# A gated attention layer and an expert layer on one core: the first stage's features and gather done by halves, the second half's projections moved into the next stage, and the unread products ahead of the first weights left out

## The reference

```python
# layer 1: attention with 16 heads of 64, gated by a top-32 choice of tokens
q, k, v = split(x @ w_qkv.T, 3)                     # INNER = 1024 each
dots = einsum('bhid,bhjd->bhij', q, k) * 64 ** -0.5
f = layernorm(q.mean(heads)) * ln_g + ln_b          # q_mean: 64 features a token
scores = gelu(f @ w1.T + b1) @ w2.T + b2            # one number a token
gate = sigmoid(scores where in the top 32 of its batch, else -1e9)   # else 0
attn = softmax(dots * gate[:, None, :, None] * gate[:, None, None, :])
x = layernorm(x + (attn @ v) @ w_out.T + b_out)

# layer 2: causal attention with 16 heads of 8, then 8 experts, top 2
x1 = x + mla(rmsnorm(x) * g1)                       # causal softmax
h = rmsnorm(x1) * g2
logits = h @ gate_w; combine = softmax of the top 2 of 8
y = x1 + sum_e combine[e] * (silu(h @ w1[e]) @ w2[e])
x = layernorm(x + y)
```

## Time and profile before

| | us |
|---|---|
| median of 3 timed runs | 706.88 |
| the 3 runs | 701.70, 706.88, 715.31 |
| the profiled execution, its own time | 699.82 |
| its span, first to last instruction | 698.1 |
| PE busy | 645.9 (93%) |
| DVE, ACT, POOL busy | 491.2, 419.5, 256.5 |
| end of the first block (the copy of delta on DVE) | 73.8 |
| mean granted clock of TensorE | 0.976 |

### The profile page before, as it was taken

The page is one execution under the profiler, slowest core; times in us unless marked ns, Lnnn a source line. Parts: engine busy times, 40 slices in busy tenths (PEclk is TensorE's granted clock), DMA queues, the critical chain, the costliest instruction groups (busy, mean ns, idle before and its releaser), DMA issues.

```text
span 698.1 us, 13992 instructions
## 1 busy us (share of the span) xinstructions
PE 645.9 (93%) x5388; PEld 429.9 (62%) x5388; DVE 491.2 (70%) x1043; ACT 419.5 (60%) x753; POOL 256.5 (37%) x321
## 2 busy tenths in 40 slices
PE   7689689889899999999999999999999999989985
PEld 2367444455456666666666766767676667756765
DVE  2557456865777778877887788768777877764775
ACT  2543254666577666766685768666857575664432
POOL 3632301221243344343532543343334343533433
PEclk9899798999999999999999999999999999999999
DMA  8500000000000000000000000000000000000000
GB/s 318 178 0 32 1 1 1 2 1 1 1 1 2 1 1 1 16 2 1 1 17 1 1 2 16 1 1 3 16 1 1 2 17 1 1 1 16 1 16 15
DMA packets 9923, 12.15 MB, mean 17 GB/s; under 512 B 1593, under 2 KB 8194, under 8 KB 9602
## 3 DMA queue, kind: packets, MB, share of 16 engines
q1 hardware_dynamic: 9106, 11.25, 4.8%
q10 hardware_dynamic: 752, 0.01, 0.1%
HBM read 9.16 MB, written 2.10 MB: 16 GB/s over the span
## 4 chain that ended last, share of the span: by engine, by line
PE 69%; DVE 10%; ACT 5%; issue 3%; POOL 2%; POOLq 0%; ACTq 0%; DVEq 0%
PE turn L964 15%; PE turn L957 11%; PE psV L1017 11%; PE psW L1005 9%; PE psS L990 6%; PE turn L919 5%; PE turn L909 3%; DVE negmax L1198 3%; PE psS L979 2%; ACT prob L1117 2%; PE turn L927 2%; ACT X L1036 1%; PE turn L938 1%; DVE qs L1207 1%; PE turn L872 1%
## 5 line engine op out<-in xcount | busy, mean ns | idle before, releaser
L1117 ACT ACTIVATE prob<-psW 128x1024 f32<-128x1024 f32 (+1 forms) x192 | 182.9, 953 | 109.5 <-PE psW L1005 109.1
L1198 DVE TENSOR_REDUCE negmax<-psS 128x2 f32<-128x1024 f32 (+2 forms) x249 | 198.7, 818 | 31.5 <-PE psS L990 31.0
L841 POOL TENSOR_SCALAR_AFFINE_SELECT prob<-prob 128x512 f32<-128x512 f32 x128 | 80.0, 638 | 280.0 <-ACT prob L1117 280.0
L1258 DVE SCALAR_TENSOR_TENSOR late<-late,turn 128x512 f32<-128x512 f32 x128 | 87.5, 684 | 66.3 <-ACT late L1087 65.6
L964 PE MATMUL turn<-wexp,late 128*128 128x128 f32 x1024 | 128.0, 278 | 1.5 <-DVE late L1258 1.3
L964 PEld LDWEIGHTS turn<-wexp,late 128*128 128x128 f32 x1024 | 119.6, 192 | 9.6 <-issue 6.0
L1087 ACT ACTIVATE late<-turn 128x512 f32<-128x512 f32 x128 | 76.4, 598 | 60.7 <-PE turn L957 57.9
L1005 PE MATMUL psW<-qT,kT 26*128 26x256 f32 (+2 forms) x512 | 93.1, 400 | 8.9 <-ACT prob L1117 8.1
L849 POOL TENSOR_TENSOR late<-late 128x512 f32<-128x512 f32 x63 | 80.6, 1280 | 45.7 <-DVE late L1277 45.7
L979 PE MATMUL psS<-kT,qT 24*128 24x256 f32 (+1 forms) x498 | 90.7, 400 | 1.7 <-DVE negmax L1198 1.6
L1017 PE MATMUL psV<-prob,va 128*32 128x512 f32 (+3 forms) x1024 | 91.0, 450 | 0.2 <-POOL prob L841 0.2
(11 more groups left out here) (260 smaller groups left out, 900.8 us busy)
## 6 DMA issues: line engine op xcount, KB each, us to landing
XT<-in_xT SPq DMA_DIRECT2D x4, 512.0 KB, 6.7
X<-in_x SPq DMA_DIRECT2D x1, 2048.0 KB, 15.8
out<-late SPq DMA_DIRECT2D x8, 256.0 KB, 2.2
WQKV<-in_wqkvT SPq DMA_DIRECT2D x1, 1024.0 KB
late<-in_w SPq DMA_DIRECT2D x1, 1024.0 KB, 9.6
WQKV<-in_wqkvT SPq DMA_DIRECT2D x2, 256.0 KB, 3.7
late<-in_woutT SPq DMA_DIRECT2D x1, 512.0 KB
base_all<-base_rows SPq DMA_DIRECT2D x1, 512.0 KB, 3.8
```

Of the source, the lines that this page charges most:

```text
L841: pool.affine_select(out=blk, in_=blk, compare_op=ALU.is_ge, fill=0.0, base=0, pattern=[[0, 4], [1, P]], channel_multiplier=-1).then_inc(s ...
L1117: A(into, src, ACT.Exp).then_inc(s["exp_ready"], 1)
L1198: last = V.tensor_reduce(negmax[:, u % 2, c, 2 * p:2 * p + 2], scores_in(b, n)[:, :, HALF * i:HALF * i + P * (c + 1)], AX, ALU.max, negate ...
L1258: V.scalar_tensor_tensor(out=hid[:, e % 2, k, :], in0=tanh[:, n % 2, :], scalar=1.0, in1=bank("hidden", b, n)[:, :], op0=ALU.add, op1=ALU. ...
```

## The change

First block:

- **Features by halves.** `features`, the copies, squares, variances and gate rows go by 256 tokens of each batch: eight steps t (first halves of all batches, then second halves) in place of four. The first half's variance, root and reciprocal run while the second half's products are made. w1g waits for three of the small loads only (`ld_w1`); the other four are waited for later (`ld_gate`). A root table is loaded ahead on ACT. 12 unread products (IN_GATE) stand on PE behind the transposes of the value weights and ahead of the scores' product.
- **Split gather.** Half 0 is gathered (16 of the 32 multiplications, L331 before), then its base rows, queries, keys and scores follow; half 1 is gathered after those scores. ACT copies its Xg and xm, and its base rows have a product, a copy and two DMAs of their own. POOL adds batches 3, 5, 6 and 7, DVE the other four.
- **The other half's projections** (16 query and key multiplications, 2 of values) leave the first block, with the 10 unread products at L377. They become six steps `half parts` between `apply` of batch 0 and `apply` of batch 1 in the second block, in the rotation of the three turn banks, emptied by ACT. For that WQKV, XT, Xg and Xc lie in the memory of `prob`, which the second block first writes at its first weights.

Second block: 11 of the 28 places in UNREAD_AT go, all those below 0; some places in the tables are moved by 0.2 to 2 slots; the last two experts' sums of the last batch are done on DVE alone (it was the last one only).

```diff
-            for j in range(B // 2):
-                if j >= 1 and j + 1 < B // 2:
-                    features(j + 1)
-
-                pe.wait_ge(f_sb, 2 * j + 2)
-                mm(bank[6][rows_of(j), :], ones64[:, :], sq[:, j % 2, :], start=True, stop=True,
+            for t in range(B):
+                h, j = divmod(t, B // 2)
+                if t >= 1 and t + 1 < B:
+                    features(t + 1)
+
+                pe.wait_ge(f_sb, 2 * t + 2)
+                mm(var_in[h][rows_of(j), 0:HALF], ones64[:, :], sq[:, t % 2, 0:HALF], start=True, stop=True,
                    tile_position=(0, 2 * GH * j)).then_inc(v_done, 1)
...
+            pe.wait_ge(masks, 2)
+            pe.wait_ge(g_used, 1)
+            unread(IN_GATE)
...
+            gather(0)
+            pe.wait_ge(xs_sb, 1)
+            base_rows(0)
...
+            pe.wait_ge(w1_scaled, 1)
+            gather(1)
...
-            values(0, (bank[7], bank[5]))
-            other = [bank[k] for k in (2, 3, 0, 1)]
-            queries_keys(1, other, range(2))
-            pe.wait_ge(s_shift, 1)
-            queries_keys(1, other, range(2, 4))
-
-            pe.wait_ge(qk1_sb, 1)
-            for i in range(IN_SOFTMAX):
-                mm(bank[2][:, :], keep["identb"][:, :], keep["maskb"][:, :], start=True, stop=True)
+            pe.wait_ge(xm_ready, 1)
+            base_rows(1)
...
-            dve.wait_ge(ld_gate, 16 * 5)
-            dve.wait_ge(ld_zero, 32)
-            dve.wait_ge(consts, 1)
-            V_.tensor_scalar(w1g[:, :], w1raw[:, :], gcol[:, :], None, ALU.mult)
-            V_.tensor_scalar(w2sel[:, :], w2sel[:, :], w2col[:, :], None, ALU.mult).then_inc(wc_ready, 1)
+            dve.wait_ge(ld_w1, 16 * 3)
+            V_.tensor_scalar(w1g[:, :], w1raw[:, :], gcol[:, :], None, ALU.mult).then_inc(w1_ready, 1)
...
+            for n in range(NH):
+                rows = slice(HB * n, HB * n + HB)
+                sp.wait_ge(base_sb, n + 1)
+                sp.dma_start(keep["rows"][rows, :], base[:, n, :]).then_inc(base_out[n], 16)
+                sp.wait_ge(base_out[n], 16)
+                sp.dma_start(base_all[:, rows, :], keep["rows"][rows, :].unsqueeze(0).broadcast_to([P, HB, D])
+                             ).then_inc(base_in[n], 16)
...
+WARM, IN_GATE, BY_POOL = 7, 12, (3, 5, 6, 7)
...
-OF_GROUP = {"keys": -12.05, "queries": -13.6, "shift": -4.1, "again": -3.1, "values": -6.75}
+OF_GROUP = {"keys": -12.05, "queries": -13.4, "shift": -4.1, "again": -3.45, "values": -5.4}
...
-GATE_AT, SUM_AT, ADD_AT = 1.0, 1.21, 2.02
+GATE_AT, SUM_AT, ADD_AT = 1.0, 1.21, 1.32
...
+    ("half parts", 0): -40.25, ("half parts", 1): -40.15, ("half parts", 2): -40.05, ("half parts", 3): -39.95,
...
 UNREAD_AT = [
-    -11.2, -10.2, -9.2, -8.2, -7.2, -6.2, -5.2, -4.2, -2.2, -1.2, -0.2, 1.8, 3.8, 5.8, 7.8, 9.8, 11.8, 13.8, 15.8,
...
-                    if (b, n) == (B - 1, NE - 1):
+                    if b == B - 1 and n >= NE - 2:
```

More of the change, by code:

```diff
@@ L298, in _ @@
             last.then_inc(wvo_ps, 1)
-            pe.wait_ge(ld_next, 16 * len(keep["loads"]))
-            mm(bank[5][:, 0:2 * D], keep["wd"][:, :], keep["wu"][:, :, :], start=True, stop=True).then_inc(wqk_ps, 1)
-            def unread(count):
-                for i in range(count):
-                    mm(bank[6][:, :], keep["identb"][:, :], keep["maskb"][:, :], start=True, stop=True)
-            pe.wait_ge(masks, 2)
             for i in range(TOPK // 8):
@@ L312, in _ @@
             unread(6)
+            pe.wait_ge(ld_next, 16 * len(keep["loads"]))
+            mm(bank[5][:, 0:2 * D], keep["wd"][:, :], keep["wu"][:, :, :], start=True, stop=True).then_inc(wqk_ps, 1)
             pe.wait_ge(wvo_sb, 1)
@@ L350, in _, with gather @@
[L350 to L353 removed]
+            def gather(n):
+                pe.wait_ge(gr_ready, n + 1)
+                for b in range(HB * n, HB * n + HB):
+                    o = (2 * TOPK + 1) * (b % HB)
+                    for c in range(C):
+                        last = mm(bank[4 + n][:, o:o + 2 * TOPK + 1], X[:, C * b + c, :], GR[:, C * b + c, :],
+                                  start=(c == 0), stop=(c == C - 1))
+                last.then_inc(xs_ps, 1)
@@ L887, in _ @@
                     pe.wait_ge(s["half_T"], 2)
+                    for i in range(4, 6):
+                        wait_free(pe, "half parts", 0, i)
                     for k in range(H):
```

301 lines of the change are left out of this document (161 added, 140 removed).

## The result

| | before | after |
|---|---|---|
| median, us (15 runs each) | 706.88 | 698.05 |
| lowest and highest | 700.40, 715.31 | 696.30, 699.49 |
| the profiled execution, own time | 699.82 | 698.13 |
| its span | 698.1 | 696.0 |
| mean granted clock | 0.976 | 0.969 |

The ratio of the times is 0.9903, 95% interval 0.9879 to 0.9927: 6.9 us less (5.2 to 8.6) at 706.88 us. The longest executions of the kernel before, over 1.5% above its fastest, are left out of this ratio and not of the median. The two profiled executions differ by 2.1 us of span only, since the one of before was shorter than all of its timed runs.

A forecast was written before the change was run, and what follows sets the result against it. PE was read as busy almost throughout from 200 us, so gains must come ahead of the first weights at 110 us, plus the tail. Terms 3.7 + 3.7 - 0.7 + 0 + 2.3 + 0.4 = 9.4 us gave 697.5 us, range 687 to 706.

The forecast's parts named there:

- Gate stage: Start to scores on DVE: features by halves, loads decide, scores at 26.1 us against 29.78; 3.7 us gained.
- upper end: Gate stage: the bias lands before X, so the scores come at 24.5 us; a gain of 5.3 us.
- Split gather: First block: all 64 gather passes took 7.33 us, the path now has 32 of them; 3.7 us gained.
- End of the block: First block's end, old clock: POOL's additions end it at 74.5 us, not 73.8; 0.7 us lost.
- The six new steps: Second block's start: moved projections covered by PE's idle time; 0, bounds 1.3 us lost and 1.5 gained.
- the clock stays low: Lower bound for the six new steps at the second block's start: 1.3 us lost.
- Unread products: Between scores and first weights: 22 products go, PE keeps 12.7 us of work; 2.3 us gained.
- the clock falls between the scores: Rival, from the first scores on: a lower clock takes the 2.3 us back; 4.4 gained, 702.5 us, chance 0.17.
- Tail: Last experts' sums: DVE's sum no longer stands behind POOL's addition; 0.4 us gained.
- Tables: Moved places of steps and POOL's additions: PE does the same work, so 0, up to 5 us gained.
- more than the sum: Rival, long stretch: PE's waits of 7.2 and 3.9 us go by half; 14.9 gained, 692 us, chance 0.22.
- So I subtract the same gain from the median: Whole kernel: the 9.4 us taken off the profiled execution (690.4 us) also come off the median (697.5 us).

The follow-up runs named there:

- a_no_gate: The changed kernel without the 12 unread products ahead of the scores' product (IN_GATE = 0); median 696.53 us, ratio 0.9879 to the kernel before.
- a_gather_whole: The changed kernel with the gather of half 1 put back directly behind that of half 0; median 699.3 us, ratio 0.9937 to the kernel before.
- a_share: The changed kernel with batch 7's base row added by DVE and not by POOL; median 697.25 us, ratio 0.9873 to the kernel before.
- a_apply_first: The changed kernel with apply of batch 1 ahead of the six half parts; median 697.0 us, ratio 0.9898 to the kernel before.
- b_unread_out: The kernel before without its 11 places of unread products ahead of the first weights; median 710.02 us, ratio 1.0083 to the kernel before.
- a_unread_back: The changed kernel with the 11 places of unread products put back; median 693.38 us, ratio 0.9823 to the kernel before.
- c_three: The changed kernel with the 11 unread places back, IN_GATE = 0 and batch 7 added by DVE; median 693.16 us, ratio 0.9850 to the kernel before.
- a_tables_old: The changed kernel with the old places in the tables and of the additions; median 701.07 us, ratio 0.9980 to the kernel before.
- b_again: The kernel before run once more, unchanged; median 705.3 us, ratio 0.9986, profiled execution 712.11 us.
- b_warm: The kernel before with ten unread products in place of six behind the last round of the top 32; median 702.61 us, ratio 0.9981.
- b_two_covers: The kernel before with its two PE waits of the gate stage covered by unread products; median 702.66 us, ratio 0.9964.
- a_warm_end: The changed kernel with 14 unread products behind the last product of the first block; median 697.27 us, ratio 0.9885 to the kernel before.

## Why the prediction was right in its sum and wrong in its terms

The forecast was 697.5 us, the median is 698.05. It was reached by terms of 9.4 us, of which the profiled executions show 2.1 of span; that the two agree is luck, as the terms show.

- **Gate stage, forecast 3.7 us: 4.5.** Right that the halves bring the scores forward, wrong in what comes last. The loads did not decide, as the upper end had it: the value transposes started at 20.57 us, ahead of the 21.2 that was taken from X's landing, with no wait beside them. The unread products cost 0.7 us of it (a_no_gate).
- **Split gather, forecast 3.7 us: between 1.2 and 3.3 at the block's start, not shown in the time.** The step that says too much is "the path now has 32 of them". Without the split the second base rows, for which POOL waits, came only 1.0 us later, no more than the gather itself; and part of a_gather_whole's 3.34 us is low clock. And what is gained ahead of the barrier opens PE's wait there: in after the clock took all of it back before the first score.
- **End of the block, forecast POOL's third addition near 67.1 us: 65.97.** Right, 1.1 us early, 0.85 of it the scores'. a_share shows that POOL ends the block: with one addition less it starts 1.12 us earlier.
- **The six new steps, forecast 0 with 1.3 lost as the worst: 3.3 lost.** The step that failed read "74.1 + 0.8 + 5.8 + 0.8 = 81.5", 7.4 us, at full clock. In after these steps took 10.5 (66.50 to 77.01 us): the half parts 7.6 (5.74 and 1.88), the first apply 2.04. In a_gather_whole, with the clock at 1.00, they took 7.7. So 2.8 of the 3.3 us are a low clock behind the 3.18 us in which PE had waited for POOL. What followed was as forecast: six passes of `qkv` took 2.17 us, 0.36 each for the "0.33". The bound "the clock stays low" priced only the offset's lag. That this lag is real shows in a_apply_first, where the way to batch 1's offset is 3.3 us shorter.
- **Unread products, forecast 2.3 us gained: 2.4 lost in the stretch, 5.7 in the time by the ratio.** The sign was wrong: the first exponential came at 108.39 us instead of near 101, and the rival *the clock falls between the scores* was true in kind: forecast 5 us of difference to the sum, measured 4.7. Its detail was other than thought: the clock is low at the first score in both kernels of the pair, and the products bring it back 10 us sooner. PE, read as the bound with 16.77 of 17.3 us, was not what the products kept from the scores.
- **On the rule of the Trainium skill** ("TensorE: Matmul & The Clock Gate", section "HAM oscillation — how this bites in real kernels"): it puts such falls down to idle gaps of PE. In after, idle gaps did precede each fall at the start of the second block, the 3.18 us at the barrier and the waits between 80 and 88 us. By it alone the removal would have cost nothing, since no gap opened between the scores; the pair b_unread_out and a_unread_back and the row of 11.29 busy us at 0.51 say that it did. Nor does the length of a gap decide here: behind 2.11 us of idleness the first eight passes ran at half clock (a_share, 2.04 us), behind 2.12 us they and the half parts ran at full clock (c_three):

```profile
66.50 1.12 PE L883 MATMUL turn<-delta,SR 32*128 32x128 f32 x8 [2.12 <-PEq L75]
67.56 3.84 PE L894 MATMUL turn<-prob 128*128 128x128 f32 x32
```

- **Tail, forecast 0.4: 0.3.** The last sum started 0.10 us behind the last product instead of 0.44:

```profile
683.93 3.75 PE L989 MATMUL turn<-wexp,late 128*128 128x128 f32 x32
...
687.78 1.13 DVE L1302 SCALAR_TENSOR_TENSOR late<-turn,comb,late 128x128 f32<-128x128 f32 x4 [0.66 <-PE turn L989]
```

- **Tables, forecast 0 with up to 5: 3.0 by the medians, 5.4 by the ratios** (a_tables_old), not placed in the profile. That is the greater part of the 6.9 us of the ratio of the whole change. "PE does the same work, so 0" is the step: the same work ran at another clock in part of the executions. PE's waits for exponentials were 6.6 us instead of 7.2, so *more than the sum* did not come by those waits.
- **From the profile to the median.** "So I subtract the same gain from the median" is the step that made the sum come out. The profiled execution should have taken 690.4 us; it took 698.13. The timed runs of before lie from 700.40 to 715.31, 0.6 to 15.5 us above their profile, those of after from 1.8 below to 1.4 above. So 7.1 of the 8.8 us of the medians are the end of this spread, and 1.7 the difference of the profiled executions' own times. In one execution of 712 us (b_again) it was a gather at 0.50. For the runs between 700 and 712 us no profile of the kernel before itself exists, but its edited versions show two more places: in the executions of 711 us (b_warm) and 722 us (b_unread_out) 4.1 us went in a fall some 30 us behind the first exponential and 3.0 near the end, and in the one of 705 us (b_two_covers) the 3.0 alone. In all nine profiles of the changed kernel's family the clock is at 1.00 from 30 to 50 us behind the first exponential, and from 90 to 80 us ahead of the end. Which part of the change ended the spread stays open: it is neither the split (a_gather_whole, 3.2 us) nor the 12 gate products (a_no_gate, 2.1 us). The old tables bring a part of it back (7.0 us); they place the steps in which the two later falls lie, but the one profile of a_tables_old, its shortest execution, has neither. Covers in before's gate stage take a part away (8.9 us against 12.2 beside it). For the falls in the first block the shorter waits of the gate stage by halves are the likeliest cause; that is argued, not shown, and two executions of the changed kernel's family (a_warm_end, a_apply_first) fell there too.

## What to carry to other kernels

A gain that ends at a wait of PE for another engine can be paid back behind it, if PE's clock falls there: price the work behind the barrier at half clock as a bound, or give PE less to gain and nothing to wait for. Products that nobody reads were worth 5.7 us between small products that follow a gap, and cost 0.7 us of the path in the gate stage; only a run with and one without tells which. An edit that is removed from the changed kernel shows its worth only if both profiles ran at the same clock up to that place: look at the windows before the difference is read. And where the timed runs spread over 15 us, a profile of the shortest one can't tell what the median will gain.

## What the runs showed of the hardware

PE's clock doesn't come back by work alone at once: 13.78 of 13.8 us of 128-row passes of 65 columns were run at 0.50 (the gather in b_again), and 11.29 of 11.3 us of scores and small products at 0.51 (after, from 88.7 us). In a_unread_back, where pairs of 512-column bf16 products lie ahead of and between the same scores, the clock was 0.88 from 87.5 to 90 us and 1.00 from there. It also stayed at 0.50 for 12 us in which PE was busy for 11.67 (b_warm, 144 to 156 us). With the same code the fall came in some executions and not in others: in the changed kernel's first block nowhere from 0 to 60 us in its own profile, at 42 us in a_warm_end and a_apply_first, whose code up to that place is the same.
